# Five unread products and a re-ordered prologue in a two-sequences-at-a-time transformer layer

## What is computed

```python
Q, K, V = split_heads(x @ Wq.T + bq), split_heads(x @ Wk.T + bk), split_heads(x @ Wv.T + bv)  # 16 heads of 8
scores = Q K^T / sqrt(8);  scores = where(j > i, -inf, scores) - (i - j)
x = layernorm(x + (softmax(scores) V) @ Wo.T + bo)
h = silu((x @ w1.T) * s1) * ((x @ w2.T) * s2)          # 128 -> 512
h = gelu((h @ h1.T) * t1);  h = gelu((h @ h2.T) * t2)   # 512 -> 512, twice
x = layernorm(x + (h @ w3.T) * s3)                      # 512 -> 128
```

## Time and profile before

| | before |
|---|---|
| median of three runs (lowest, highest) | 764.84 us (763.87, 765.87) |
| profiled execution, span from first to last instruction | 763.0 us |
| PE busy, share of the span | 721.0 us, 94% |
| VectorE busy | 590.4 us, 77% |
| ScalarE busy | 551.7 us, 72% |
| GpSimd busy | 509.7 us, 67% |
| mean granted TensorE clock | 0.957 of full speed |

### The profile page before, as it was taken

One profiled execution on the slowest core, in us unless ns is written; L12 is line 12 of the kernel. 1 busy time (PEld: TensorE's weight loads), 2 busy tenths in 40 slices (PEclk: granted clock), 3 DMA queues, 4 the chain that ended last, 5 costly groups with the idle time before them and its releaser, 6 DMA issues.

```text
span 763.0 us, 18187 instructions
## 1 busy us (share of the span) xinstructions
PE 721.0 (94%) x5993; PEld 496.8 (65%) x5993; DVE 590.4 (77%) x2761; ACT 551.7 (72%) x876; POOL 509.7 (67%) x616
## 2 busy tenths in 40 slices
...
PEclk8566899999999999999999999999999999999997
...
GB/s 238 170 35 32 111 46 9 133 30 121 45 108 55 45 105 17 128 37 114 51 75 78 17 133 30 120 46 111 52 64 86 17 131 21 119 33 24 25 1 29
DMA packets 56367, 54.18 MB, mean 71 GB/s; under 512 B 28048, under 2 KB 36496, under 8 KB 56272
## 3 DMA queue, kind: packets, MB, share of 16 engines
...
q10 hardware_dynamic: 288, 0.08, 0.0%
...
## 4 chain that ended last, share of the span: by engine, by line
PE 57%; ACT 13%; DVE 12%; issue 8%; SPq 4%; DMA 3%; POOL 2%; POOLq 0%; DVEq 0%; ACTq 0%
PE ps L586 18%; PE ps L592 15%; DVE ps L964 7%; ACT pt L809 5%; PE ps L631 5%; PE ps L690 5%; PE ps L671 3%; PE ps L605 3%; ACT sg L859 3%; PE ps L699 2%; DVE m L964 2%; ACT L809 2%; PE ps L612 1%; DMA sums<-raw 1%; ACT k_hi L800 1%
## 5 line engine op out<-in xcount | busy, mean ns | idle before, releaser
L964 DVE CUSTOM_DVE_ANT_0 ps<-ps,causal 128x256 f32<-128x256 f32 (+1 forms) x928 | 297.4, 392 | 21.6 <-PE ps L634 21.4
L1108 POOL TENSOR_SCALAR_AFFINE_SELECT pt<-pt 128x512 f32<-128x512 f32 x256 | 160.6, 637 | 97.7 <-ACT pt L809 92.5
L1151 POOL TENSOR_TENSOR hlo<-hf,hhi 128x512 fp32r<-128x512 f32 x128 | 163.9, 1286 | 91.9 <-ACT hhi L894 90.4
L809 ACT ACTIVATE pt<-ps 128x768 f32<-128x768 f32 x256 | 194.7, 811 | 26.8 <-PE ps L673 24.4
L884 ACT ACTIVATE hf<-ps,vec_sb 128x512 f32<-128x512 f32 x128 | 86.2, 684 | 99.7 <-PE ps L592 99.7
L586 PE MATMUL ps<-hhi,h_hi 128*128 128x512 f32 x496 | 146.0, 415 | 0.3 <-ACT hhi L894 0.3
L592 PE MATMUL ps<-hlo,h_hi 128*128 128x512 f32 x496 | 139.5, 398 | 1.2 <-POOL hlo L1157 0.7
L964 DVE DVE_READ_ACCUMULATOR2_ANT m<- 128x1 f32 x928 | 130.4, 141 | 0.0
L592 PEld LDWEIGHTS ps<-hlo,h_hi 128*128 128x128 f32 x496 | 93.3, 188 | 28.8 <-POOL hlo L1157 6.3
L690 PE MATMUL ps<-pt,vst 128*32 128x256 f32 (+1 forms) x2048 | 106.5, 337 | 0.1
L586 PEld LDWEIGHTS ps<-hhi,h_hi 128*128 128x128 f32 x496 | 85.3, 188 | 20.5 <-ACT hhi L894 0.7
...
## 6 DMA issues: line engine op xcount, KB each, us to landing
...
den<-sums SPq DMA_DIRECT2D x128, 32.0 KB, 1.9
...
```

The costliest lines, as they stand in the source:

```text
L809: nc.scalar.activation(pt[u][:, c:c + 2, :], ps[:, first:last + 1, 0:3 * P], ACT.Exp).then_inc(t_free.sem, 1)
L964: part = nc.vector.tensor_tensor_reduce(ps[:, bank, cols], ps[:, bank, cols], mask, 1.0, LOWEST, ALU.add, ALU.max, m32[b][:, max_col(c + e ...
L1108: nc.gpsimd.affine_select(out=diag, in_=diag, compare_op=ALU.is_ge, fill=0.0, base=0, pattern=[[0, 2], [0, 2], [1, P]], channel_multiplier ...
L1151: nc.gpsimd.tensor_tensor(h_lo[layer % 2][:, m, :], hf[:, n % 4, :], h_hi[layer % 2][:, m, :].bitcast(F32), ALU.subtract).then_inc(hlo_rea ...
```

## The change

All of it lies in the fill; the slots' lists are the same.

1. A new PE step `warm`: a float32 product of the value weights with the query rows that the start has loaded (128x128 by 128x512), written to the bank of `pv` and read by nobody. Five of them stand among pair 1's heads. The first waits until `araw` of pair 0's second sequence has read that bank.
2. `w_hi`, `w_lo` and `w_mx` do one piece a step, eleven steps each, spread over the lists.
3. The five lists of the fill stand in a new order. The table for GELU is loaded early, not between pair 0's and pair 1's exponentials; the second load of x goes ahead of the weights.

```diff
 FIRST_PIECES = 5
+WARM_EARLY = 0
...
 PE_FILL = [
...
+    ("s1", 1, 2, 1, 1), ("warm", 0, 0), ("st", 0, 0, 1), ("s1", 1, 3, 0, 1), ("s1", 1, 3, 1, 1), ("warm", 1, 0),
+    ("st", 0, 1, 1), ("s1", 1, 4, 0, 1), ("warm", 2, 0), ("s1", 1, 4, 1, 1), ("warm", 3, 0), ("s1", 1, 5, 0, 1),
...
+                        elif kind == "warm":
+                            if s[1] == 0:
+                                pe.wait_ge(qrows_in, 16)
+                                pe.wait_ge(v_in, 32)
+                            if s[1] == WARM_EARLY:
+                                raw_ready.wait(pe, 0, 2)
+                            pe.matmul(ps[:, PVB, :], wv_sb[:], sg[:, 0, :], start=True, stop=True)
...
                     elif kind == "w_hi":
-                        if q == 0:
+                        name, cols, buf = staged[s[1]]
+                        if s[1] < FIRST_PIECES:
                             act.wait_ge(ffn_in, 16 * (1 + FIRST_PIECES))
                         else:
                             act.wait_ge(ffn2_in, 16 * (len(staged) - FIRST_PIECES))
-                        for name, cols, buf in staged[parts_of[q]]:
-                            nc.scalar.copy(w_hi[name][:, cols], buf).then_inc(split_hi, 1)
+                        nc.scalar.copy(w_hi[name][:, cols], buf).then_inc(split_hi, 1)
...
                     elif kind == "w_mx":
-                        for n in range(len(staged))[parts_of[q]]:
-                            name, cols, _ = staged[n]
+                        n = s[1]
+                        name, cols, _ = staged[n]
...
                     elif kind == "w_lo":
-                        for n in range(len(staged))[parts_of[q]]:
-                            name, cols, buf = staged[n]
-                            pool.wait_ge(split_hi, n + 1)
+                        n = s[1]
+                        name, cols, buf = staged[n]
+                        pool.wait_ge(split_hi, n + 1)
```

More of the change, by code:

```diff
@@ L88 @@
[L88 to L92, removed]
@@ L93 @@
-    ("ghi", 1, 0), ("tanh", 3, 0), ("ghi", 2, 0), ("ghi", 3, 0), ("araw", 1, 1), ("gelu", 1, 0, 0), ("hhi", 1, 0, 0),
-    ("gelu", 1, 1, 0), ("hhi", 1, 1, 0), ("gelu", 1, 2, 0), ("hhi", 1, 2, 0),
+    ("qhi", 0, 0), ("qhi", 1, 0), ("rows", 0), ("w_hi", 0, 0), ("w_hi", 1, 0), ("table", "gelu", 1), ("qhi", 0, 1),
+    ("w_hi", 2, 0), ("qhi", 1, 1), ("w_hi", 3, 0), ("w_hi", 4, 0), ("w_hi", 5, 0), ("exp", 0, 0, 0),
+    ("exp", 0, 1, 0), ("exp", 0, 2, 0), ("exp", 0, 3, 0), ("exp", 0, 4, 0), ("exp", 0, 5, 0), ("exp", 0, 6, 0),
@@ new lines @@
+    ("w_hi", 6, 0), ("exp", 0, 7, 0), ("exp", 1, 0, 0), ("w_hi", 7, 0), ("exp", 1, 1, 0), ("exp", 1, 2, 0),
+    ("exp", 1, 3, 0), ("exp", 1, 4, 0), ("exp", 1, 5, 0), ("exp", 1, 6, 0), ("exp", 1, 7, 0), ("araw", 1, 0),
+    ("exp", 0, 0, 1), ("exp", 0, 1, 1), ("w_hi", 8, 0), ("exp", 0, 2, 1), ("exp", 0, 3, 1), ("w_hi", 9, 0),
+    ("exp", 0, 4, 1), ("exp", 0, 5, 1), ("qhi", 0, 2), ("exp", 0, 6, 1), ("qhi", 1, 2), ("w_hi", 10, 0),
+    ("exp", 0, 7, 1), ("lnnorm", 1, 0), ("exp", 1, 0, 1), ("x1hi", 0), ("x1c", 0), ("exp", 1, 1, 1),
@@ L95 @@
+    ("exp", 1, 2, 1), ("tanh", 0, 0), ("exp", 1, 3, 1), ("exp", 1, 4, 1), ("tanh", 1, 0), ("exp", 1, 5, 1),
+    ("ghi", 0, 0), ("tanh", 2, 0), ("ghi", 1, 0), ("exp", 1, 6, 1), ("tanh", 3, 0), ("exp", 1, 7, 1), ("ghi", 2, 0),
+    ("ghi", 3, 0), ("araw", 1, 1), ("gelu", 1, 0, 0), ("gelu", 1, 1, 0), ("hhi", 1, 0, 0), ("hhi", 1, 1, 0),
+    ("gelu", 1, 2, 0), ("hhi", 1, 2, 0),
 ]
 DVE_FILL = [
-    ("rows", 0, 0), ("rows", 1, 0), ("qlo", 0, 0), ("qlo", 1, 0), ("ones", 0), ("vadd", 0), ("smax", 0, 0, 0),
@@ L98 @@
-    ("smax", 0, 1, 0), ("smax", 0, 2, 0), ("smax1", 1, 0, 0, 0), ("smax", 0, 3, 0), ("qlo", 0, 1),
-    ("smax1", 1, 0, 1, 0), ("smax", 0, 4, 0), ("smax", 0, 5, 0), ("smax1", 1, 1, 0, 0), ("qlo", 1, 1),
-    ("smax1", 1, 1, 1, 0), ("smax", 0, 6, 0), ("smax", 0, 7, 0), ("vadd", 1), ("smax1", 1, 2, 0, 0),
[11 rows of a table removed]
-    ("mTc", 1, 1), ("mTl", 1, 1), ("w_mx", 1), ("qlo", 1, 2), ("vadd", 2), ("araw", 0, 1), ("x1lo", 0),
-    ("gate", 0, 0), ("gmul", 0, 0), ("gate", 1, 0), ("gmul", 1, 0), ("gate", 2, 0), ("gmul", 2, 0),
+    ("rows", 0, 0), ("qlo", 0, 0), ("rows", 1, 0), ("qlo", 1, 0), ("ones", 0), ("vadd", 0), ("smax", 0, 0, 0),
@@ new lines @@
+    ("smax", 0, 1, 0), ("smax", 0, 2, 0), ("smax1", 1, 0, 0, 0), ("smax1", 1, 0, 1, 0), ("qlo", 0, 1),
+    ("smax1", 1, 1, 0, 0), ("smax1", 1, 1, 1, 0), ("smax", 0, 3, 0), ("smax", 0, 4, 0), ("smax", 0, 5, 0),
[8 rows of a table added]
+    ("smax1", 1, 0, 0, 1), ("mTc", 0, 1), ("smax1", 1, 0, 1, 1), ("mTl", 0, 1), ("w_mx", 2, 0), ("arec", 0, 0),
[4 rows of a table added]
+    ("mTl", 1, 1), ("w_mx", 4, 0), ("w_mx", 5, 0), ("w_mx", 6, 0), ("qlo", 1, 2), ("vadd", 2), ("x1lo", 0),
+    ("araw", 0, 1), ("gate", 0, 0), ("gmul", 0, 0), ("w_mx", 7, 0), ("w_mx", 8, 0), ("gate", 1, 0), ("w_mx", 9, 0),
@@ L114 @@
+    ("w_mx", 10, 0), ("gmul", 1, 0), ("gate", 2, 0), ("gmul", 2, 0),
 ]
 POOL_FILL = [
-    ("w_lo", 0), ("sel", 0, 0, 0), ("sel", 0, 1, 0), ("sel", 0, 2, 0), ("sel", 0, 3, 0), ("sel", 0, 4, 0),
-    ("sel", 0, 5, 0), ("xbo", 0), ("sel", 0, 6, 0), ("sel", 0, 7, 0), ("sel", 1, 0, 0), ("sel", 1, 1, 0),
-    ("sel", 1, 2, 0), ("sel", 1, 3, 0), ("sel", 1, 4, 0), ("sel", 1, 5, 0), ("sel", 1, 6, 0), ("sel", 1, 7, 0),
-    ("sel", 0, 0, 1), ("sel", 0, 1, 1), ("amul", 0, 0), ("sel", 0, 2, 1), ("sel", 0, 3, 1), ("amul", 1, 0),
@@ new lines @@
+    ("sel", 0, 7, 0), ("w_lo", 5, 0), ("sel", 1, 0, 0), ("sel", 1, 1, 0), ("sel", 1, 2, 0), ("sel", 1, 3, 0),
+    ("sel", 1, 4, 0), ("sel", 1, 5, 0), ("sel", 1, 6, 0), ("sel", 1, 7, 0), ("sel", 0, 0, 1), ("sel", 0, 1, 1),
+    ("amul", 0, 0), ("xbo", 0), ("amul", 1, 0), ("sel", 0, 2, 1), ("w_lo", 6, 0), ("sel", 0, 3, 1),
+    ("sel", 0, 4, 1), ("w_lo", 7, 0), ("w_lo", 8, 0), ("sel", 0, 5, 1), ("rstd", 1, 0), ("sel", 0, 6, 1),
+    ("sel", 0, 7, 1), ("sel", 1, 0, 1), ("w_lo", 9, 0), ("w_lo", 10, 0), ("sel", 1, 1, 1), ("sel", 1, 2, 1),
```

32 lines of the change are left out of this document (15 added, 17 removed), and 60 rows, old and new, of tables (DVE_FILL, PE_FILL).

## The result

The changed kernel takes 758.18 us, the median of six runs (757.72 to 761.99), beside 764.41 us (six runs, 763.62 to 765.87) for the kernel before on the same chip: a ratio of 0.9925, 95% interval 0.991 to 0.994. It is 6.2 us faster; I had said 763.1, range 760.3 to 768.8. Two further series of the unedited change are among the experiments; over all 17 runs the median is 758.71 us, from 757.5 to 762.0, so the first series flatters it a little.

What follows compares the result with a forecast made beforehand. The fill's end, the slots' first product at 97.77 us, was taken to set the time, with PE the bound in pair 0's `pv` stretch. Terms +2.1 + 0.3 − 4.4 + 0.3 = −1.7 gave 763.1 us, range 760.3 to 768.8.

Steps and rivals of the forecast that it cites:

- Pair 0, up to its last `pv`: Fill up to pair 0's last `pv`: first score group moves behind three more heads, last `pv` ends later, +2.1 us.
- PE's debt: From pair 0's first to last `pv`: PE still owes two score groups and one head, 1.1 us, plus 0.3 waiting.
- the start: Load of x ahead of the weights: put at nothing, since the first score product waits for the stacked keys.
- My fourth rival: Pair 0 costs nothing because heads pace the fill: +2.1 falls to 0, time 761.0 us; chance 0.20.
- The five products: Between pair 0's last `pv` and `wo`: products lie beside SP's chain and cost little, `wo` later by +0.3 us.
- From `wo` to `x1t`: Fill behind `wo`: products and projections run at full instead of half clock, −4.4 us.
- From `x1t` to the slots: Feed-forward at the fill's end: two blocks of `w_mx` mostly fill VectorE's waits, +0.3 us left.
- The slots: After the fill: their lists are not touched, so no change in their length was predicted.
- the first (the clock rises late): Pair 0: clock rises only with its last two `pv`, +6.0 instead of +2.1 us, time 767.0; chance 0.20.
- The second (the products do not hold the clock): Fill: the five products neither hold nor raise the clock, 2.9 us above the first rival, 769.9; chance 0.11.

Runs made afterwards that it cites:

- the mirror: The kernel before with nothing but the new order of pair 0 on PE (up to its last `pv`) and of its first maxima on VectorE: 766.67 us, ratio 1.0032.
- The block run: The changed kernel with the weights' splitting back in the two blocks of before, products and all other lists as changed: 767.01 us, ratio 1.0021.

## Why the prediction was wrong

I had given 0.33 to a gain of more than 2.3 us, and the time lay 2.1 us below my range. The step that failed is pair 0: I priced the moved score group as a delay, +0.7 up to the first `pv` and +1.4 behind it, and two of the three profiles show no delay of the pair. Of the 4.9 us by which I was off, that step makes 2.5, the products' term 0.7, and 1.4 is scatter of the slots. Term by term, against the first profile:

*Pair 0, up to its last `pv`: +2.1; measured −0.4 (+1.3 and −0.1 in the other two profiles).* This term failed, and it makes 2.5 of the fill's error of 3.3 us. I priced three heads at 0.76 us, from the last four heads ahead of the first score group, where PE and VectorE take turns; in the stretch as a whole VectorE is the bound, and the three heads added 40.20 − 16.71 − (39.01 − 17.11) = 1.6 us, not 2.3. And the first `pv`, for which I took +0.7, came 0.6 earlier against the first score product (the mirror shows that the order alone does this): two score groups fewer stand ahead of it on PE, and the three heads lie where VectorE is the bound. That is 1.3 of the 2.5. From there to the last `pv` I took +1.4 for PE's debt; it was +0.6 (13.1 us for 12.5; 13.3 and 14.3 in the other two profiles, by the moment of the clock's rise): 0.8 more. The last 0.4 is the start, which I had put at nothing because the first score product waits for the stacked keys. In the kernel before it stands right behind `qq` of pair 1, without idle time between, and `qq` had waited for the load of x:

```profile
15.08 2.05 PE L605 MATMUL ps<-xT,wq_sb 128*128 128x512 f32 x2 [4.21 <-DMA xT<-in_x]
17.11 0.59 PE L631 MATMUL ps<-ks,qs 32*128 32x256 f32 x4
```

It starts at 17.1 us in the three profiles with old lists and at 16.2 to 17.3 (the middle one 16.8) in the eleven with new ones, so the earlier load may be worth 0.3 us; no run tried it alone. My fourth rival, pair 0 costs nothing (chance 0.20), came nearest, with 761.0 us still 2.8 above the result.

*The five products: +0.3; measured −0.4.* The mechanism is right: 1.10 to 1.13 us each, beside SP's chain. My count of PE's work behind `araw`, 10.6 us, was too high: from 60.47 to the start of the idle time ahead of `wo`, 69.98 − 0.65 = 69.33, it was 8.9, as heads and groups overlap more than I allowed: they filled 2.4 us, not 4.2. So SP's chain, not PE, set `wo`, against my sign for it. With ten products it was PE.

*From `wo` to `x1t`: −4.4; measured −4.5.* Right in size and cause: without the products it is 14.2 us, with them 10.4, and 11.5 where the clock fell for a moment. The block run shows that the term rests on the single pieces too, on VectorE's maxima as well as on `rstd`, which alone I had named.

*From `x1t` to the slots: +0.3; measured +0.4* (12.4 us for 12.0; 12.3 in both other profiles).

*The slots: 0; measured −1.4 in the first profile, +0.1 and −1.2 in the others.* From the slots' start to the end of the span, profiles with old lists took 665.2, 665.4 and 664.4 us, the one without products 665.2, and all of this study lie between 663.7 and 665.5 with no order by lists, but for the one with products from the start (668.1), where many slots are a little longer and the cause is open. So none of it can be put down to the change; the first profile drew a short one and that of before a long one. In the second profile 1.2 us are a fall of the clock near 700 us (last section). The slots' own 1.4 us is thus scatter that I could not have summed.

Of the rivals, the first (the clock rises late) did not come: the moment does vary, in the change by 3.8 us, but the latest was 55.4, not 65, and cost 1.2 us. The second (the products do not hold the clock) is refuted by the run without them. The page rule that I set beside it, the Trainium skill, "TensorE: Matmul & The Clock Gate", section "Why this matters for your kernels", puts drops down to idle gaps between bursts. The block run comes nearest to it: half clock followed on PE busy 3.08 of 5 us, idle 1.73 of them in one piece. The fall at 56 to 57 us in the run with three products does not fit: in the 3 us ahead of it PE was busy 2.61, idle 0.39 us in all, with `pv` and small products. Nor does the fall at 63.1 without the products: the longest idle time of PE in the 4 us ahead was 0.22 us. The measurement decides: avoiding gaps is not enough here.

What the parts are worth, as the runs have it: the new lists without products 1.2 us; products on the old lists, −1.8; pair 0's new order on the old lists, −2.9; the new lists and products with pair 0 in the old order, −0.4, and with the weights in blocks, −2.3; all together, by the three ratios, 4.4 to 5.7.
